# Reciprocal roots of two LayerNorms and an RMS norm: from Newton chains on VectorE to powers on GpSimd

## The reference

```python
# x: (4, 1024, 256); D = 256; mod gives sa, ca, ga, sb, cb, gb for each batch
h = layernorm(x) * (1 + ca) + sa
norm = jnp.linalg.norm(h, axis=-1, keepdims=True) * D ** (-0.5)
xn = rms_scale * h / (norm + 1e-8) * split_scale
K = sigmoid(xn @ W_K); u, g_in, g_out = split(xn @ W_ugg, 3)
u = u * sigmoid(g_in) * (1.0 - K)
# outputs: the recurrence s_t = K_(t-1) * s_(t-1) + u_t over the tokens
x = x + ga * ((outputs * sigmoid(g_out)) @ W_out + h)
h = layernorm(x) * (1 + cb) + sb
# top 2 of 8 experts for each token: gelu(h @ W1[e] + b1[e]) @ W2[e] + b2[e]
x = x + gb * (sum over the two of weight * expert(h))
```

## Time and profile before

| | |
|---|---|
| median of 3 runs | 828.49 us (826.09 to 829.99) |
| profiled execution, its own time | 831.49 us |
| profiled execution, span | 829.7 us |
| mean granted TensorE clock, share of full | 0.934 |
| attention part, PE's first main matmul | 23.36 us |
| start of group g = 6 and g = 7 on PE | 247.29 us and 280.00 us |

### The profile page before, as it was taken

One profiled execution on the slowest core, in us unless ns is written; L12 is line 12 of the kernel. 1 busy time (PEld: TensorE's weight loads), 2 busy tenths in 40 slices (PEclk: granted clock), 3 DMA queues, 4 the chain that ended last, 5 costly groups with the idle time before them and its releaser, 6 DMA issues.

```text
span 829.7 us, 16986 instructions
## 1 busy us (share of the span) xinstructions
PE 717.6 (86%) x4850; PEld 660.5 (80%) x4850; DVE 565.9 (68%) x1725; ACT 405.1 (49%) x1024; POOL 406.2 (49%) x312
## 2 busy tenths in 40 slices
PE   4669999898899993479999899979889989979992
PEld 2558888787678872379999899979889979979992
DVE  6898899998989776755554755537666456485561
ACT  6425545444443432146655555636555555555650
POOL 1255527683835635555434544435455544544443
PEclk9869999999989997579999999999999989999996
DMA  7081011220202015333436344545443542524432
GB/s 281 2 280 52 16 36 66 77 101 6 75 7 72 26 53 198 126 102 67 67 66 164 54 72 68 116 103 165 110 105 63 114 114 50 122 53 64 72 71 40
DMA packets 50164, 72.55 MB, mean 87 GB/s; under 512 B 5792, under 2 KB 41964, under 8 KB 49968
## 3 DMA queue, kind: packets, MB, share of 16 engines
q0 software_dynamic: 16480, 27.28, 17.8%
q1 hardware_dynamic: 33616, 44.46, 17.2%
HBM read 48.85 MB, written 22.87 MB: 86 GB/s over the span
## 4 chain that ended last, share of the span: by engine, by line
PE 36%; DVE 22%; DMA 18%; issue 13%; POOL 6%; ACT 2%; another core or an unknown queue 1%; DVEq 1%; POOLq 0%; SPq 0%; ACTq 0%
DMA out_x<-ysb,tokb 17%; PE mm L750 14%; PE yb L904 7%; PE mm L894 7%; PE yb L775 5%; POOL gbr L534 3%; DVE ysb L1255 2%; POOL out_x L539 2%; DVE ob L999 2%; DVE ysb L1259 1%; DVE nt L931 1%; DVE rt L1033 1%; DVE SL L233 1%; DVE mm L996 1%
## 5 line engine op out<-in xcount | busy, mean ns | idle before, releaser
L727 ACT ACTIVATE h<-mm,b1T 128x256 f32<-128x256 f32 (+1 forms) x288 | 134.6, 467 | 199.2 <-PE mm L894 112.5
L539 POOL DMA_INDIRECT out_x<-ysb,tokb x68 | 110.5, 1625 | 205.9 <-DVE ysb L1259 157.2
L1232 DVE TENSOR_TENSOR hl<-h,hh 128x256 fp32r<-128x256 f32 (+1 forms) x288 | 122.4, 428 | 125.4 <-ACT hh L728 97.9
L904 PE MATMUL yb<-SH,hh 128*128 128x256 f32 x544 | 160.1, 294 | 29.2 <-DVE hl L1232 29.1
L894 PE MATMUL mm<-fh,SH 128*128 128x256 f32 x576 | 165.2, 287 | 8.4 <-DVE fl L1199 6.9
L894 PE MATMUL mm<-fl,SH 128*128 128x256 f32 x576 | 163.8, 284 | 0.0
L894 PE MATMUL mm<-fh,SL 128*128 128x256 f32 x576 | 163.5, 284 | 0.0
L904 PE MATMUL yb<-SL,hh 128*128 128x256 f32 x544 | 155.4, 286 | 0.0
L904 PE MATMUL yb<-SH,hl 128*128 128x256 f32 x544 | 155.0, 285 | 0.0
L728 ACT ACTIVATE hh<-mm,b1T 128x256 fp32r<-128x256 f32 (+1 forms) x288 | 134.0, 465 | 0.0
L904 PEld LDWEIGHTS yb<-SH,hh 128*128 128x128 f32 x544 | 105.2, 193 | 32.0 <-DVE hl L1232 32.0
(11 more groups left out here) (205 smaller groups left out, 1191.4 us busy)
## 6 DMA issues: line engine op xcount, KB each, us to landing
xin<-disp_x SPq DMA_DIRECT2D x74, 132.0 KB
wraw<-in_L_ffn_W SPq DMA_DIRECT2D x8, 1024.0 KB
h2all<-in_L_ffn_W SPq DMA_DIRECT2D x8, 1024.0 KB
xb<-in_L_attn_x SPq DMA_DIRECT2D x8, 512.0 KB, 7.1
out_x<-x2b SPq DMA_DIRECT2D x8, 512.0 KB, 3.0
mb<-mod_rows SPq DMA_DIRECT2D x3, 768.0 KB, 6.2
wraw<-in_L_attn_W_ugg SPq DMA_DIRECT2D x1, 1536.0 KB, 10.1
gbr<-mod_rows,xm POOLq DMA_INDIRECT x74
```

The source lines that it names most:

```text
L539: e.indirect_dma_start(out=out_rows, out_offset=bass.IndirectOffsetOnAxis(ap=tokb[:, j:j + 1], axis=0), in_=ysb[:, j, :], in_offset=None, ...
L727: e.activation(h32[:, f % 2, c_], mm[f % 4][:, c_], ACT.Gelu_apprx_tanh, bias=bias)
L904: i = e.matmul(yb[0][:, j * D:(j + 1) * D], a[:, f, j * 128:(j + 1) * 128], b[:, f, :], start=(f == 0 and j == 0 and t == 0), stop=(f == N ...
L1232: e.tensor_tensor(hl[:, f, w_], h32[:, f % 2, w_], hh[:, f, w_].bitcast(F32), ALU.subtract)\
```

## The change

Three of the four kinds of root leave DVE. `ln1_stats` and `ln2_stats` (the latter but for the last group, which keeps the old chain) now end with mean and variance in `mv` (`means`), and `ln1_norm` is gone. POOL takes over: `ln1_scales(g)` and `ln2_scales(g)`, 8 instructions each with one power, and `rms_scales(g)`, 12 instructions with two powers. Every power is a TENSOR_TENSOR on 128 x 4 numbers with a tile `pw` of exponents and is followed by one Newton step; the instructions of a chain wait for each other by the semaphore `pool_own`.

```diff
@@ pool_program
+            e.memset(pw[:, 0, :], -0.5).then_inc(S["powers_made"], 1)
+            e.memset(pw[:, 1, :], -1.0).then_inc(S["powers_made"], 1)
+            def rsqrt(v, y, a):
+
+                link(e, e.tensor_tensor(y, v, pw[:, 0, :], ALU.pow), "pool_own")
+                link(e, e.tensor_tensor(a, y, y, ALU.mult), "pool_own")
+                link(e, e.tensor_tensor(a, a, v, ALU.mult), "pool_own")
+                link(e, e.tensor_scalar(a, a, -0.5, 1.5, ALU.mult, ALU.add), "pool_own")
+                link(e, e.tensor_tensor(y, y, a, ALU.mult), "pool_own")
+
+            def ln_scales(q, y, ready):
+                v, a, m = (pt[:, q, i, :] for i in range(3))
+                e.tensor_scalar(m, mv[:, q, :, 0], -1.0, None, ALU.mult)
+                link(e, e.tensor_scalar(v, mv[:, q, :, 1], 1e-5, None, ALU.add), "pool_own")
+                rsqrt(v, y[:, 0, :], a)
+                e.tensor_tensor(y[:, 1, :], m, y[:, 0, :], ALU.mult).then_inc(S[ready], 1)
+            def rms_scales(g):
+                v, y, a, d = (pt[:, 2, i, :] for i in range(4))
+                e.wait_ge(S["powers_made"], 2)
+                e.wait_ge(S["h_squared"], g + 1)
+                past(e, "rms_ready", g)
+                past(e, "xn_ready", g - 1)
+                link(e, e.tensor_scalar(v, ss[:, g % 2, :], 1.0 / D, 1e-34, ALU.mult, ALU.max), "pool_own")
+                rsqrt(v, y, a)
+                link(e, e.tensor_tensor(d, v, y, ALU.mult), "pool_own")
+                link(e, e.tensor_scalar(d, d, 1e-8, None, ALU.add), "pool_own")
+                link(e, e.tensor_tensor(y, d, pw[:, 1, :], ALU.pow), "pool_own")
+                link(e, e.tensor_tensor(a, d, y, ALU.mult), "pool_own")
+                link(e, e.tensor_scalar(a, a, -1.0, 2.0, ALU.mult, ALU.add), "pool_own")
+                e.tensor_tensor(rin[:, g % 2, :], y, a, ALU.mult).then_inc(S["rms_ready"], 1)
+            ln1_scales(0)
+            rms_scales(0)
             for g in range(NG):
                 if g == 0:
+                    ln1_scales(1)
                     ln1_modulate(1)
                     gate_wout(0)
+                    ln1_scales(2)
+                    rms_scales(1)
+                else:
+                    if g + 2 < NG:
+                        ln1_scales(g + 2)
+                    if g + 1 < NG:
+                        rms_scales(g + 1)
                 gate_h(g)
...
                 if g >= 1:
+                    ln2_scales(g - 1)
                     ln2_modulate(g - 1)
@@ dve_program
+            def means(src, q, ready):
+
+                for j in range(4):
+                    i = e.bn_stats(bst[:, q, j, :], src[:, j, :])
+                yield from lk(e, i, "dve_a")
+                for j in range(4):
+                    i = e.bn_aggr(mv[:, q, j, :], bst[:, q, j, :])
+                i.then_inc(S[ready], 1)
...
             weights_low(0, 1)
-            weave(ln1_norm(0))
             weights_low(1, 0)
...
                 elif g + 2 < NG:
-                    weave(ln1_stats(g + 2), ln1_norm(g + 1))
-                elif g + 1 < NG:
-                    weave(ln1_norm(g + 1))
+                    weave(ln1_stats(g + 2))
```

More of the change, by code:

```diff
@@ L36 @@
     "mod_loaded1", "mod_loaded2", "zero_made", "pads_zeroed", "w_high", "w_low", "wout_gated", "b1_copied",
-    "x_stats", "x_scaled", "h_ready", "h_squared", "rms_ready", "xn_ready", "xn_turned", "xn_high", "xn_low",
+    "x_moments", "x2_moments", "powers_made", "x_stats", "x_scaled", "h_ready", "h_squared", "rms_ready", "xn_ready", "xn_turned", "xn_high", "xn_low",
     "hx_ready", "main_done", "in_gated", "k_ready", "out_gated", "u_gated", "w_ready", "scanned",
@@ L84, in build @@
         rsn = sb(ctx, "rsn", [128, 2, 2, 4])
+        pw = sb(ctx, "pw", [128, 2, 4])
+        pt = sb(ctx, "pt", [128, 3, 4, 4])
         ss = sb(ctx, "ss", [128, 2, 4])
@@ L449, in token_columns, with ln1_scales, ln2_scales @@
                        channel_multiplier=0).then_inc(S["meta_made"], 1)
+            def rsqrt(v, y, a):
[10 more added lines that the diff above has]
+                e.tensor_tensor(y[:, 1, :], m, y[:, 0, :], ALU.mult).then_inc(S[ready], 1)
+            def ln1_scales(g):
+                e.wait_ge(S["powers_made"], 2)
+                e.wait_ge(S["x_moments"], g + 1)
+                past(e, "x_stats", g)
+                past(e, "x_scaled", g - 1)
+                ln_scales(0, rsn[:, g % 2, :, :], "x_stats")
+            def ln2_scales(g):
+                e.wait_ge(S["x2_moments"], g + 1)
+                past(e, "x2_stats", g)
+                past(e, "x2_scaled", g - 1)
+                ln_scales(1, rsn2[:, g % 2, :, :], "x2_stats")
+            def rms_scales(g):
+                v, y, a, d = (pt[:, 2, i, :] for i in range(4))
+                e.wait_ge(S["powers_made"], 2)
+                e.wait_ge(S["h_squared"], g + 1)
[9 more added lines that the diff above has]
+                e.tensor_tensor(rin[:, g % 2, :], y, a, ALU.mult).then_inc(S["rms_ready"], 1)
             def ln1_modulate(g):
@@ L946, in moments @@
                     .then_inc(S[ready], 1)
+            def means(src, q, ready):
[5 more added lines that the diff above has]
+                i.then_inc(S[ready], 1)
             def ln1_stats(g):
                 e.wait_ge(S[X_LOADED[g % 3]], 16 * (g // 3 + 1))
[L950 to L960, removed]
+                past(e, "x_stats", g)
+                yield from means(xb[:, g % 3, :, :], 0, "x_moments")
             def weights_low(part, k):
@@ L1020, in ln2_stats @@
                 e.wait_ge(S["x2_ready"], g + 1)
+                past(e, "x2_stats", g)
+                if g < NG - 1:
+                    yield from means(x2b[:, g % 2, :, :], 1, "x2_moments")
+                    return
                 yield from moments(x2b[:, g % 2, :, :], 1, rsn2[:, g % 2, :, :], "x2_scaled", g - 1, "x2_stats")
@@ L1156, in dve_program @@
                 recur(g, 1)
-                if g == 0:
-                    weave(ln1_norm(1))
                 weave(*([ln2_stats(g - 1)] if g >= 1 else []), *([place(g - 2), gate_weights(g - 2)] if g >= 2 else []))
```

## The result

The changed kernel takes 848.0 us (median of 4 runs, 843.97 to 850.59) where the kernel before, run beside it, takes 829.24: 1.0223 times as long, 95% interval 1.0164 to 1.0281. The forecast of 826.2 us was wrong in size and in sign; 848 lies outside its range. Of the rivals only C, the dear power, points this way, and the time lies beyond its 837.4 us too. The profiled execution took 850.59 us, its span is 848.8.

The account below looks back on a forecast made before the run. DVE, which PE waits for, was taken as the bound, with at most 18.0 us to win; POOL would take over. Loop -6.1 and head +3.8 us sum to -2.3, so 828.5 becomes 826.2 us; range 816 to 838.

Parts of the forecast that it names:

- C: Rival, chance 0.25: powers on POOL are dear and the kernel gets slower; at 1.0 us over a multiplication, +8.9, 837.4 us.
- c: Total time of the 28 small instructions added to POOL's loop: 6.3 us without extra power cost, 7.1 with it.
- The head: Before PE's first matmul: the norm on POOL loses time to DVE's weight subtractions, so that matmul comes 3.8 us later.
- the ring POOL, ACT, POOL: Attention loop: POOL's ln2_scales, ACT's ln2_scale, POOL's ln2_modulate in sequence set the pace; groups of 33.8 (even) and 36.1 us (odd).
- I choose 0.2: Small powers on POOL: each taken to cost 0.2 us more than a multiplication, from 2.3 ns a number times twenty steps.
- p: Extra cost of one POOL power over a multiplication, bounded between 0 and 1.0 us.
- 14p - 5.1: Whole kernel: formula for the change in time in us by the power's extra cost; zero at 0.36.
- Until gate_h(3) at 140.50 POOL has room; I leave it there.: Attention loop before 140.50 us: POOL's added instructions fit its room, so gate_h(3) keeps its start.
- The lock: In the head, POOL's small instructions and DVE's two-input subtractions keep each other out; without it, 3.5 us better.
- Group 6: Attention part: PE sets the pace with 32.7 us, plus 1.6 for the lower clock after standing idle.
- DVE's busy time of the part down by 70 us: Attention part, profile of the changed kernel: DVE's busy time falls by 70 us as the root chains leave it.
- Elsewhere, 0: Head's LayerNorm statistics of x, the 30 to 52 us stretch, last LayerNorm and expert part: no effect, 0 us.

Follow-up runs that it names:

- e12: The kernel before with dead powers, multiplications and one-input steps added on POOL in the head; powers of 1, 4, 16, 64 numbers took 0.60, 1.04, 2.90, 11.40 us.
- e3: The changed kernel with every power replaced by a linear step of the same length as a multiplication; 1.0067 of the kernel before.
- e7: The changed kernel with the first power of each root issued twice, the second as dead work; 1.0419 of the kernel before.
- e2: The changed kernel with DVE waiting for POOL's norm of group 0 before subtracting the second weight matrix; 1.0181 of the kernel before.
- e9: The changed kernel with the norm of h and group 0 back on DVE and ln2_scales ahead of ln1_modulate; 822.31 us, 0.9897 of the kernel before.
- e11: The changed kernel with only x2's LayerNorm roots left on POOL, ahead of ln1_modulate, the other roots on DVE; 823.40 us, 0.9890 of the kernel before.

## Why the prediction was wrong

Three steps failed: the price of a power (chosen 0.2 us over a multiplication, measured 0.84), the price of the links (c without the powers, 6.3 us against 7.8), and the room that POOL was given ahead of gate_h(3), where the runs show it on the path already. The head was under-sized besides. From gate_h(3) on the structure held. The trace gives each number at group 7, where the prediction said 277.7 (273.9 and the head's 3.8) and 297.26 was measured, 19.6 us more.

- **POOL becomes the bound through the ring POOL, ACT, POOL.** Right. POOL runs without a break from gate_h(3) on, the hand-over costs 2.19 us (2.15 predicted), ACT's ln2_scale is released by POOL, and PE starts 5.15 us after ln2_scale (179.18 to 184.33; 5.1 predicted). That DVE gives up the pace is right too.
- **"I choose 0.2".** This step failed first, and alone it turns the sign of the formula. A power costs 1.04 us against 0.20, p = 0.84. The argument, 2.3 ns a number times twenty steps, had the form of an estimate but nothing to rest on: the 2.3 ns hold for a long row of numbers, and e12 shows 150 ns for each further number in a power. The prediction's own formula, 14p - 5.1, gives +6.7 us with this p, 835 us: slower, but 13 us short of the 848. The upper end that I had taken for p, 1.0, did hold it.
- **c.** The links were mis-sized as well: mostly 0.28 us from start to start of dependent multiplications where 0.26 was taken, 0.28 to 0.33 for one-input ones where 0.22 was. A LayerNorm's chain takes 3.09 us (150.89 to 153.98) or 3.06 (from 176.09), the norm's 4.99 (to 158.97), so c = 11.1 against 7.1; 2.6 of the 4.0 are the powers. The rings from ln2_scale to ln2_scale are 38.04 and 40.49 us instead of 33.8 and 36.1 (179.18, then 217.22 and 257.71). Three rings: 12.9 us of the 19.6. e3, which takes only the powers out, gives back 10.9 at group 7, 2.3 of them in the head, where the formula's fourteen at 0.84 are 11.8: for the powers alone its slope was right. e7 adds three to each ring and costs 18.1, where the formula's three rings would take nine at 1.10, 9.9, and two in the head 2.2: more than three rings are bound.
- **"Until gate_h(3) at 140.50 POOL has room; I leave it there."** Wrong. ACT waits for POOL already in an earlier ring, in the changed kernel at 101.89:

```profile
101.89 1.59 ACT L693 ACTIVATE h2all<-x2b,rsn 128x256 f32<-128x256 f32 x3 [5.49 <-POOL rsn L468]
```

  The part of the ring that I started at 140.50 starts at 150.89, with ln1_scales(5). Of these 10.4 us 6.2 are the head; the other 4.2 are lost in the rings before. In e7 the delay grows from group 2 on, which shows the same by a second way. POOL does still stand idle in that stretch, for DVE's statistics:

```profile
78.41 0.23 POOL L465 TENSOR_SCALAR pt<-mv 128x4 f32<-128x4 f32 x1 [5.09 <-DVE mv L1012]
...
112.31 0.24 POOL L465 TENSOR_SCALAR pt<-mv 128x4 f32<-128x4 f32 x1 [3.44 <-DVE mv L1012]
```

  DVE makes these at the start of a group, behind xn_low. So the ring runs over DVE as well there (statistics, POOL's roots, ACT's ln2_scale, xn_low, statistics), and idle time on POOL was no sign of room.
- **The head.** The lock is right: it appears in the two instructions and goes away in e2. Its size is not: 6.2 us instead of 3.8. The norm starts 1.0 us later (16.29 for 15.29), since the LayerNorm's root before it, with a power too, is late (ACT starts on it at 9.72 for 8.85), and DVE's subtraction starts 0.9 us later than said (17.63 for 16.7). And with a first power of 1.03 us POOL is only at its third instruction by then, not its fifth: ten wait for the lock or stand behind it, and the eight after the two waits take 3.1 us (21.23 to 24.36) where six were to take 1.6. The Trainium skill, page "SBUF — State Buffer", section "Who interferes with whom", has whoever starts first keep the other out; the trace agrees (1.77 and 1.65 us for four numbers, each until half of DVE's 3.55 us is over). Here each POOL multiplication waited for one of DVE's two. The 2.27 us that the prediction set beside this are those of a one-input instruction; the two-input ones behind it in the same chain took 2.20 and 2.32 us (at 51.50 and 53.73).
- **Group 6.** 34.40 us against 32.7 + 1.6: right, with the clock at 0.95 over the group.
- **DVE's busy time of the part down by 70 us.** By windows from the first main matmul to 312 us before and 330 us after it fell from 253.78 to 195.91, by 58. The prediction added up durations, and those of neighbouring instructions overlap: summed, DVE's durations fall from 290 to 216 us, by 74.
- **Elsewhere, 0.** The span from group 7 on is 1.8 us longer. This is within what the traces of nearly the same work differ by here (549.6 to 555.8 us), and no experiment was made on it.

Put together: head 2.3 more than said, rings before gate_h(3) 4.2, three rings 12.9, group 6 0.1, which make the 19.6 but for rounding. The sign hung on p alone in the formula. But for p = 0 the formula gives -5.1 us, and e3 measured +5.6 (1.0067 of 831.22). So the other sizes, 0.06 us on each of 24 links, the "room" before group 3 and the head, turn the sign without any power.

A gain of the kind that was expected of DVE's relief can be had: e9 and e11 are about 9 us faster than the kernel before, with few small instructions on POOL and the root of x2 ahead of the large ones. In the changed kernel it went into ACT's wait for a root that stands in POOL's queue behind 7 us of work that is less urgent, and behind 8 us of roots for later groups.

## What to carry to other kernels

Work that leaves a busy engine for an idle-looking one is paid where it stands in the new engine's order: look for the ring that runs through that engine, add up its length for each group, and start that sum at the first group, not where the trace of before happens to show the bound. Price an operation that no row shows by its upper bound when the sign depends on it, or measure it alone first, at two sizes. And move the one root that the waiting engine needs, ahead of the large pieces, before moving all: in this kernel 8 of 28 instructions at the early place gained 1.1%, all of them at the late place cost 2.2%.

## What was unexpected of the hardware

- A TENSOR_TENSOR with a power on GpSimd costs by the number: 0.60, 1.04, 2.90 and 11.40 us for 1, 4, 16 and 64 fp32 numbers a partition, against 0.19 to 0.32 us for a multiplication.
- Dependent small instructions on GpSimd start mostly every 0.28 us for multiplications and 0.28 to 0.33 for one-input steps, of which some 0.08 lie between end and start.
- Small dependent GpSimd instructions and wide VectorE ones alternate one for one: each of two four-number multiplications waited for one of two subtractions of 1536 numbers (1.77 and 1.65 us for 0.20).
